# First projection slot of an attention and FP4 feed-forward kernel: dequantisation, identity and second weight set moved behind it

## The reference

```
x = query                                            # b=4, s=4096, h=2048
mixed = x @ Wqkv.T            ; split into q, k, v of 16 heads of 128
attn = softmax(q k^T / sqrt(128)) ; ctx = attn v
x = layernorm(x + (ctx @ Wproj.T + bproj))
w_gu, w_down = dequant_fp4(packed codes, fp16 scales per group of 128)
gate, up = split(x @ w_gu.T)  ; h = silu(gate) * up   # inner size 5632
y = h @ w_down.T ; y = y / rms(y)
out = layernorm(x + y)
```

## Time and profile before

| | before |
|---|---|
| median of 3 runs | 4273.65 us (4271.99 to 5007.27) |
| profiled execution, its own time | 4271.61 us |
| span of its slowest core (core 2) | 4270.0 us |
| spans of all cores | 4261.4 to 4270.0 us |
| mean granted TensorE clock, all cores | 0.990 to 0.991 |
| PE busy | 4096.9 us, 96% of the span |
| DVE, ACT, POOL busy | 925.9, 1441.3, 285.7 us |

### The profile page before, as it was taken

How to read it: one execution, slowest core, us unless ns; L and a number is a source line. 1 busy time by engine, 2 the same in 40 slices (tenths; PEclk the granted TensorE clock), 3 DMA queues, 4 the chain that set the end, 5 groups by cost and what they waited for, 6 DMA issues and landing times.

```text
span 4270.0 us, 67177 instructions; the slowest of 8 cores (4261.4 to 4270.0 us)
## 1 busy us (share of the span) xinstructions
PE 4096.9 (96%) x26992; PEld 2317.2 (54%) x27392; DVE 925.9 (22%) x1351; ACT 1441.3 (34%) x1666; POOL 285.7 (7%) x419
## 2 busy tenths in 40 slices
PE   5899999999999999999799999999999999999995
PEld 2466667666666666666455444444444444444442
DVE  5112222232222322222034201012100300031103
ACT  0155555555555555556833200000000000000000
POOL 1100000000000000000023100000000000000001
PEclk9999999999999999999999999999999999999997
DMA  9945546455554645556356545447444644455332
GB/s 192 196 100 123 128 108 143 107 115 134 114 123 109 137 115 128 120 121 119 79 194 227 184 176 194 159 146 256 149 158 153 229 170 158 153 183 197 138 130 93
DMA packets 196189, 635.67 MB, mean 149 GB/s; under 512 B 49200, under 2 KB 79920, under 8 KB 158768
## 3 DMA queue, kind: packets, MB, share of 16 engines
q1 hardware_dynamic: 144576, 447.79, 30.6%
q0 software_dynamic: 51312, 183.55, 22.3%
HBM read 660.67 MB, written 119.54 MB: 183 GB/s over the span
## 4 chain that ended last, share of the span: by engine, by line
PE 93%; DMA 3%; ACT 1%; issue 1%; DVE 1%; POOL 0%; another core or an unknown queue 0%; ACTq 0%; DVEq 0%; POOLq 0%
PE pJ L289 15%; PE pC L320 11%; PE pJ L275 10%; PE pS L304 9%; PE pS L392 7%; PE pS L396 7%; PE pS L415 7%; PE pS L353 5%; PE pJ L396 4%; PE pC L392 4%; PE pC L396 4%; PE pJ L392 4%; PE pC L415 4%; PE pJ L415 4%; DMA x<-xc 2%; ACT P L487 1%
## 5 line engine op out<-in xcount | busy, mean ns | idle before, releaser
L487 ACT ACTIVATE P<-pS 128x1024 bf16<-128x1024 f32 x1024 | 1041.3, 1023 | 740.6 <-PE pS L304 727.9
L289 PE MATMUL pJ<-x,wq 128*128 128x512 bf16 x2983 | 764.0, 384 | 74.9 <-DMA ident_bf<-ident 40.0
L320 PE MATMUL pC<-V,P 128*128 128x129 bf16 x8192 | 633.7, 220 | 30.5 <-ACT P L487 23.4
L320 PEld LDWEIGHTS pC<-V,P 128*128 128x128 bf16 x8192 | 542.0, 97 | 214.2 <-issue 84.5
L304 PE MATMUL pS<-Q,K 128*128 128x512 bf16 x1827 | 561.4, 379 | 10.9
L289 PEld LDWEIGHTS pJ<-x,wq 128*128 128x128 bf16 x3072 | 302.2, 99 | 434.2 <-issue 89.8
L275 PE MATMUL pJ<-wq,x 128*128 128x256 bf16 x4096 | 514.8, 273 | 0.4
L275 PEld LDWEIGHTS pJ<-wq,x 128*128 128x128 bf16 x4096 | 400.8, 98 | 134.8
L595 DVE RECIPROCAL rcp<-pC 128x4 f32<-128x4 f32 x64 | 11.7, 183 | 1517.0 <-PE pC L320 1517.0
L392 PE MATMUL pS<-h1T,wgu 128*128 128x512 bf16 x1408 | 318.3, 379 | 0.1
L396 PE MATMUL pS<-h1T,wgu 128*128 128x512 bf16 x1408 | 318.3, 379 | 0.0
(11 more groups left out here) (69 smaller groups left out, 2750.9 us busy)
## 6 DMA issues: line engine op xcount, KB each, us to landing
wgu<-wgu_scr SPq DMA_DIRECT2D x176, 1024.0 KB, 5.8
x<-xc POOLq DMA_DIRECT2D x256, 512.0 KB, 11.1
wd<-wdn_scr SPq DMA_DIRECT2D x176, 512.0 KB, 3.3
wgu_scr<-bits SPq DMA_DIRECT2D x44, 1024.0 KB, 8.5
wdn_scr<-bits SPq DMA_DIRECT2D x44, 512.0 KB, 4.7
xr<-xrows SPq DMA_DIRECT2D x16, 1024.0 KB, 6.2
h_scr<-h1f SPq DMA_DIRECT2D x16, 1024.0 KB, 4.7
res<-h_scr POOLq DMA_DIRECT2D x16, 1024.0 KB, 7.8
```

The source lines that it names most:

```text
L289: mm = t.matmul(out, M.wq[:, pair, part, hc, h * 128:(h + 1) * 128], x[:, hc, :], start=(hc == 0), stop=(hc == HC - 1))
L320: mm = t.matmul(M.pC[:, o:o + 129], M.P[n % 3][:, h * 512 + qt * 128:h * 512 + (qt + 1) * 128], M.V[s % 2][:, 2 * p + h, l, :], start=(p = ...
L487: a.activation(out=M.P[n % 3][:], in_=M.pS[n % 2][:], func=AF.Exp, bias=0.0, scale=NORM).then_inc(S.exp_done, 1)
```

## The change

`dequant_units(c)` gives the units of block c: two each for blocks 0 to 9, then one each up to block 55, which is 66 in all. The ten units ahead of the attention are gone on VectorE and on SyncE's queue. SyncE's queue waits for 36 finished groups (the end of chunk 6 of slot 0) before its first load of codes. On GpSimd's queue the identity and the second pair's weights are issued behind chunk 8 (slot 1's first), and no longer behind chunk 0 and chunk 6. PE waits for the identity ahead of its first transpose.

```diff
-DEQ_FIRST = DEQ_UNITS - 7 * QBLOCKS
+DEQ_TWICE = DEQ_UNITS - 7 * QBLOCKS
...
+def dequant_units(c):
+
+    first = 2 * c if c < DEQ_TWICE else c + DEQ_TWICE
+    return range(first, min(DEQ_UNITS, first + (2 if c < DEQ_TWICE else 1)))
...
 def pe_ctx_transpose(t, S, M, tile):
     t.wait_ge(S.ctxt_in[tile % 2], 16 * (tile // 2 + 1))
+    if tile == 0:
+        t.wait_ge(S.ident_in, 16)
...
 def pe_program(t, S, M):
-    t.wait_ge(S.ident_in, 16)
     for _ in pe_projections(t, S, M, 0):
...
-    for u in range(DEQ_FIRST):
-        dve_dequant(v, S, M, u)
     for c in range(SLOTS * QBLOCKS):
         dve_ctx_evac(v, S, M, c)
-        if DEQ_FIRST + c < DEQ_UNITS:
-            dve_dequant(v, S, M, DEQ_FIRST + c)
+        for u in dequant_units(c):
+            dve_dequant(v, S, M, u)
...
-    g.dma_start(out=M.ident[:], in_=M.d_ident).then_inc(S.ident_in, 16)
...
-        if gc == 6:
+        if gc == CHUNKS:
+            g.dma_start(out=M.ident[:], in_=M.d_ident).then_inc(S.ident_in, 16)
             for part in range(3):
                 g.dma_start(out=M.wq[:, 1, part, :, :],
                             in_=M.d_wqkv[1, part]).then_inc(S.w1_in, 16)
...
 def sp_program(y, S, M):
+    y.wait_ge(S.proj_done, group_offset(7))
     sp_codes(y, S, M, 0)
     sp_codes(y, S, M, 1)
-    for u in range(DEQ_FIRST):
-        sp_weights(y, S, M, u)
     for c in range(SLOTS * QBLOCKS):
         sp_ctx_store(y, S, M, c)
-        if DEQ_FIRST + c < DEQ_UNITS:
-            sp_weights(y, S, M, DEQ_FIRST + c)
+        for u in dequant_units(c):
+            sp_weights(y, S, M, u)
```

## The result

The changed kernel took 4247.7 and 4245.6 us, against 4272 to 4274 us before; the ratio is 0.9939, with a 95% interval of 0.9918 to 0.9961. (Two further runs, 4465 and 4914 us, were disturbed as one of before was; all times and ratios from here on are of undisturbed runs.) So some 26 us were won where 33 were forecast, inside the range and within 2%.

A forecast was written before the change was run, and what follows sets the result against it. Slot 0 was taken as bound by transfers, the rest by PE. 58.3 us won in slot 0 less 25.1 given back made 33.2; 4271.6 - 33.2 = 4238.4, plus 2.0 for the median, about 4240 us, range 4222 to 4256.

The forecast's parts named there:

- the sum: Slot 0 to slot 1's K0: 58.3 us won in slot 0, 25.1 given back behind it, 33.2 gained.
- The start: Slot 0's first two chunks: data flows from about 4.6 us, chunk 1 complete at 48.0, its work done at 66.8.
- The middle: Slot 0, chunks 2 to 7: loads keep up, so they run at PE's pace and slot 0 ends at 164 us.
- 15.1 fits, by 1.4 us only: Slot 0: a chunk's last quarter lands 15.1 us after its buffer is free (13.0 + 1.6 + 0.5); PE wants it at 16.5.
- rival 3: Slot 0 stays tied to x: chunks 5 and 6 each 3.1 us late, 12 us less gained, 4252 us; chance 20%.
- Behind it: Slot 1's first K0: weights behind chunk 8 land at 187.1 us, so PE stands 22 us from 165.
- The clock after the stand: Slot 1's K0: PE begins at low clock after waiting for weights, 2.8 us more.
- Two units at no cost: Blocks 0 to 9: two units and the evacuation take 17 of 31.4 us of VectorE, loads hidden by 6 us; costs nothing.
- Rival 4: Short chunks: two units a block keep GpSimd from writing x descriptors, PE stands, 42 us more, 4282 us; chance 5%.
- Rival 2: Start of slot 1: weights overlap chunk 8 better or move faster; without any stand 58.3 us gained, 4216 us; chance 10%.
- rival 5: Slot 0's transfers take as long with SyncE's queue empty, so nothing changes, 4273 us; chance 3%.
- The wait of 40.0 us for the identity: Start of slot 0: the identity itself cost little, landing at 39.7 us because it stood behind chunk 0 in the queue.

The follow-up runs named there:

- the dequantisation alone: Ten units moved out of slot 0 as in the changed kernel, identity and second pair's weights loaded as in the kernel before; 4244.0 to 4245.8 us, ratio 0.9935.
- The one and the two cores: The changed kernel on core 0 alone, and on cores 0 and 1, other output rows filled with copies; 4226.2 us and 4244.9 us, one run each.

## Why the prediction was right, and where 7 us went

**Direction and mechanism: right.** Slot 0 was bound by transfers and the rest by PE. Taking ten units away freed slot 0 (the dequantisation alone gives the full gain), and the weights behind chunk 8 gave much of it back: spreading them returned 25 us, close to the 25.1 that the sum had as given back. The first scores came at 166.3 to 169.8 us, where 164 was forecast and 175 was the limit. Three signs lay a little outside what was named: PE's stand for the weights was 24.5 us on core 6 and 25.3 on core 2 (18 to 24), slot 1's K0 at 190.2 to 196.0 us (184 to 190), and PE's wait for x was 25.3 us in all of slot 0 (15 to 20).

**The start: 3 us short.** The issue of chunk 5 stands at 111.80 us and was forecast at 108.9. The sum set landings at the end of each transfer's share of the rate; the first x quarter was to land at 9.3 us and landed on core 6 of the changed kernel 9.9 us behind its issue at 2.26, at 12.2. Part of this is the rate. The sum let the engines move 170 GB/s from 4.6 us on, 2.6 MB by 20 us; on core 6 they moved 2.3 MB by then, full as they were (columns as in the earlier trace rows):

```profile
5.00:10.00 5.00, 0.00 (x0) 0.00 (x0) 0.00 (x0) 0.00 (x0) 4.16 (x8) 1.00 1.04 117
10.00:15.00 5.00, 1.86 (x4) 0.43 (x4) 0.00 (x0) 0.00 (x0) 0.00 (x0) 1.00 1.02 161
15.00:20.00 5.00, 1.87 (x4) 0.44 (x4) 0.00 (x0) 0.00 (x0) 0.00 (x0) 1.00 1.05 147
```

The missing 0.3 MB are 1.8 us. The rest may lie between a transfer's last byte and its landing, which the sum counted only as lead; no run shows it apart.

**The middle: the mis-sized term.** "15.1 fits, by 1.4 us only" rested on the 13.0 us of the earlier trace rows, the landing of a chunk that core 2 issued at 222.8 us, when core 3, its partner, had issued its own at 214.9; core 3's last quarter landed at 228.1, so the two shared only the first 5 us or so. In slot 0 both issue within a fraction of a microsecond (chunk 5 at 111.80 on core 2 and 111.75 on core 3 in the changed kernel), and chunks 5 and 6 landed in 15.6 and 16.2 us on core 2. 16.2 + 1.6 + 0.5 = 18.3 doesn't fit into 16.5: chunk 5 was late by 1.5 us, chunk 6 by 0.6. That was rival 3 in kind, at a third of the 6.2 us that it gave these two. The issue of chunk 8 came at 155.60 instead of 150.6, 2.9 us of it from the start. The one and the two cores show that a neighbour makes the difference: 12.2 us against 15.5.

**Behind it: the same term again.** From that issue to the weights 40.2 us passed, not 36.5. Chunk 8's last quarter landed 19.5 us behind its own issue on core 2, at 176.7, with the codes and the partner beside it (how the excess divides between them isn't shown); with the 3.1 us for the codes the sum had allowed 17.7 us from the first issue, and it took 21.1. The three parts and the identity took 19.1 us, where 18.8 were forecast. (The parts of the earlier trace rows landed 6.7 and 5.8 us after one another, their issues' 0.53 us counted, and not 6.2 and 5.8 as the prediction has it; the 6.2 us a part that it used holds all the same.) Together the weights were there at 195.8, not 187.1 us.

**The clock after the stand: right.** On the chain of core 2 the first five matmuls took 2.29 us where they take 1.08, the context matmuls behind them 0.87, the scores 0.85 and the next five matmuls 1.94 us, where a step later these are 0.45, 0.43 and 1.08:

```profile
199.20 0.85 PE pS L310 x2
200.05 1.94 PE pJ L295 x5
202.00 0.45 PE pC L326 x8
202.45 0.43 PE pS L310 x2
202.88 1.08 PE pJ L295 x5
```

That is 2.9 us against 2.8 forecast. The granted clock in the stand is 0.50, the 1.2 GHz level.

On core 2: 33.2, less 8.7 for the later weights and 0.2 for PE's start behind them, and 0.1 for the clock, is 24.2 us; its span fell by 24.9. So 9 us of the sum are accounted for on this core; the two times lie 6 and 8 us above the 4240 forecast.

**Two units at no cost: right**, and the reason for it incomplete. The sum named room on VectorE and on the queues, and that codes are loaded a block ahead. At three units, with room left on VectorE, the last of these no longer holds: PE is held up by the chain from a unit's end to the landing of the codes asked for behind it. Rival 4 was priced by descriptors held up by VectorE; at two units no x landing in slot 1 came with a wait of PE, and the runs with three and four units hurt through ctxg and not through x. So that mechanism cost nothing at any load tried. Landings of x in slot 1 reached 20.6 us up to 480 us on core 6, where up to 24 were forecast.

**Rival 2** (a short stand) and **rival 5** (nothing changes) fell: the stand is 25.3 us, on the lone core still 16.5. **The wait of 40.0 us for the identity** was rightly held to be worth next to nothing.

The prediction's estimate by the Trainium skill (HBM Reference, Specifications), transfers 5% shorter, would have moved the forecast the wrong way by 3 us.

## What to carry to other kernels

Where a stage is bound by transfers, move out of it what nobody needs there, but leave in it what the next stage needs at its first step, in gaps where the DMA engines have room: three parts behind chunk 8 gave back half of what ten units had won, and behind chunks 1 to 3 the same three parts cost next to nothing (PE waited 0.4 us for them). A landing time read from the trace holds for the traffic of that moment, partner core included; for a stage in which all cores load at once, read it from such a stage. Where an in-order engine works through two buffers, count how far ahead the load for a unit is asked for, and not only how long the unit takes. And the longest wait in a list can be worth nothing, when what it waits for stands in the same queue as the next thing needed.

## What the runs showed of the hardware

A core loading float32 alone moved 211 GB/s of bf16 (one execution), and 175 when its neighbour loaded too, with the DMA engines' share at 1.03 in both: the share doesn't tell the two apart. Two cores were as slow as eight.

Core 6 of the changed kernel had a stretch with PE busy throughout and a granted clock of neither level:

```profile
460.00:474.00 14.00, 14.00 (x118) 10.50 (x117) 4.71 (x3) 6.98 (x9) 0.00 (x0) 0.81 0.98 285
```

From slot 1's sixth weight load to the end this core took 4047.9 us and core 7, which had the same stretch at the same time, 4046.9; the other six, which had none, took 4043.6 to 4046.0. So core 6 became the slowest, 1.1 us over core 2. What sets the stretch off stays open.
